# A graph-attention kernel gets its node features in two layouts: projection without transposes, attention columns from raw weights, block table three batches sooner

## The reference

```python
xn = layernorm(x)
xp = (xn @ W).reshape(n, 4, 64)
a_src = einsum('nhc,hc->nh', xp, att_src); a_dst = einsum('nhc,hc->nh', xp, att_dst)
alpha = leaky_relu(a_src[src] + a_dst[dst], 0.2)          # edges, and a loop on each node
w = softmax of alpha over the edges of each target
x = x + elu(segment_sum(xp[src] * w, dst) + bias)
z = layernorm(x)
weights = z @ wr + br                                     # the upper half of the nodes is chosen by it
x = x + z + (chosen ? (gelu(z @ w1 + b1) @ w2 + b2) * weights : 0)
```

## Time and profile before

| | us |
|---|---|
| median of 3 runs | 2629.61 |
| lowest and highest of them | 2623.77 and 2631.42 |
| time of the profiled execution | 2606.92 |
| its span in the trace | 2604.8 |

### The profile page before, as it was taken

How to read it: one execution, slowest core, us unless ns; L and a number is a source line. 1 busy time by engine, 2 the same in 40 slices (tenths; PEclk the granted TensorE clock), 3 DMA queues, 4 the chain that set the end, 5 groups by cost and what they waited for, 6 DMA issues and landing times.

```text
span 2604.8 us, 32956 instructions
## 1 busy us (share of the span) xinstructions
PE 1990.1 (76%) x9573; PEld 1660.8 (64%) x9574; DVE 1581.5 (61%) x3501; ACT 715.3 (27%) x1506; POOL 1570.7 (60%) x1644
## 2 busy tenths in 40 slices
PE   8934878877877777877877877777777787787787
PEld 7723666666666666666666666666666666666665
DVE  4555666665665565665665665665565565565576
ACT  5601232222222222222222222222222222222233
POOL 2366666666666666666666666666666666666630
PEclk9967888888888888888888888988888888888888
DMA  7754444444444444444444444444444444444447
GB/s 240 225 146 121 128 136 124 129 134 127 128 135 126 131 132 127 126 136 125 129 136 126 129 134 125 130 135 129 122 135 133 122 133 131 124 136 124 125 166 302
DMA packets 155904, 364.58 MB, mean 140 GB/s; under 512 B 46725, under 2 KB 74017, under 8 KB 154594
## 3 DMA queue, kind: packets, MB, share of 16 engines
q0 software_dynamic: 76000, 210.72, 29.9%
q1 hardware_dynamic: 72690, 140.11, 16.5%
q10 hardware_dynamic: 7184, 13.41, 1.4%
HBM read 325.22 MB, written 38.89 MB: 140 GB/s over the span
## 4 chain that ended last, share of the span: by engine, by line
POOL 39%; issue 27%; PE 14%; another core or an unknown queue 8%; DVE 5%; POOLq 3%; DMA 2%; ACT 1%; DVEq 0%; SPq 0%; ACTq 0%
POOL rows L664 39%; PE ag_ps L996 7%; PE ag_ps L885 3%; DMA rows<-node_rows,ends 2%; PE y_ps L982 2%; DVE rows L1318 1%; DVE base L1517 1%; POOLq L388 1%; PE h_ps L964 1%; POOLq L684 1%; DVE oh L1278 0%; PE tr_ps L910 0%; PE xl_ps L910 0%; DMA base<-in_x 0%
## 5 line engine op out<-in xcount | busy, mean ns | idle before, releaser
L664 POOL DMA_INDIRECT rows<-node_rows,ends x1582 | 1529.8, 967 | 860.4 <-issue 583.3
L996 PE MATMUL ag_ps<-rows,oh 128*128 128x260 f32 x3518 | 1008.7, 456 | 448.0 <-DVE rows L1318 216.3
L996 PEld LDWEIGHTS ag_ps<-rows,oh 128*128 128x128 f32 x3518 | 808.4, 233 | 618.7 <-issue 275.7
L1318 DVE TENSOR_TENSOR rows<-rows,xl_ps 128x512 f32<-128x512 f32 (+3 forms) x392 | 503.0, 1345 | 29.4 <-issue 17.1
L1297 DVE TENSOR_TENSOR zz<-rows,edge_dm 128x72 f32<-128x72 f32 x98 | 22.8, 233 | 813.6 <-DMA rows<-node_rows,ends 797.6
L964 PE MATMUL h_ps<-xnT,w1s 128*128 128x256 f32 x1568 | 381.3, 392 | 37.2 <-issue 37.0
L790 ACT COPY rows<-rows 128x520 f32<-128x520 f32 x97 | 60.6, 625 | 1261.1 <-DMA rows<-node_rows,ends 1261.1
L964 PEld LDWEIGHTS h_ps<-xnT,w1s 128*128 128x128 f32 x1568 | 307.3, 197 | 93.1 <-issue 50.2
L982 PE MATMUL y_ps<-w2s,hT 128*128 128x256 f32 x1568 | 358.2, 381 | 2.4 <-ACT hT L767 1.7
L982 PEld LDWEIGHTS y_ps<-w2s,hT 128*128 128x128 f32 x1568 | 298.4, 191 | 49.6 <-issue 2.4
L1278 DVE TENSOR_TENSOR oh<-xl_ps,dloc 128x2304 f32<-128x2304 f32 x98 | 250.0, 2551 | 0.0
(11 more groups left out here) (220 smaller groups left out, 1367.7 us busy)
## 6 DMA issues: line engine op xcount, KB each, us to landing
dbc<-dst SPq DMA_DIRECT2D x97, 576.0 KB
rows<-node_rows,ends POOLq DMA_INDIRECT x1582
selfr<-node_rows SPq DMA_DIRECT2D x98, 130.0 KB
base<-in_x SPq DMA_DIRECT2D x14, 896.0 KB, 4.6
base<-in_x SPq DMA_DIRECT2D x49, 256.0 KB
ffn_rows<-yb ACTq DMA_DIRECT2D x48, 256.0 KB
node_rows<-base SPq DMA_DIRECT2D x13, 910.0 KB, 4.8
out<-base SPq DMA_DIRECT2D x4, 896.0 KB, 9.6
```

What stands on the lines that cost most here:

```text
L664: pool.indirect_dma_start(out=rows[:, b, t, :], out_offset=None, in_=table, in_offset=bass.IndirectOffsetOnAxis(ap=ends[:, b, t, 0:1], axi ...
L996: product = nc.tensor.matmul(ag_ps[b][:, 0:ROW], oh[:, b, t, :], rows[:, b, t, :], start=(t == 0), stop=False)
L1318: nc.vector.tensor_tensor(v, v, e, ALU.mult).then_inc(scaled[k], 1)
```

## The change

`x` comes a second time, as `x_turned`: for each batch 128 partitions (features) by 2 halves of 7 x 128 nodes, 7,168 B per partition like the batch of `x`. It has 4 buffers `xt` of its own. PE takes tiles of `xt` as its stationary operand; the transposes and ACT's copies of them are gone. Both loads of a batch count on one semaphore, so DVE and PE wait for both. The load of batch g+4 now waits until PE has projected batch g (`xp_ok`). W and the attention vectors are loaded first. The attention columns are made of the raw W, and `center` then takes the means off all 264 columns; it stands between the statistics and the aggregation of batch 0. The masks move to batches 7 and 8, the counting on PE to the middle of batch 8, the blocks to batch 9, POOL's fetch to its step 10, `window_edges` to batch 11, its sum on PE to the middle of batch 12, the copying out (`first_tiles`) into batch 13. `w1` and `w2` are loaded after the targets of window 0 instead of in batch 10. The batches are written out instead of looped.

```diff
         def _(sp):
             def load_x(g, q):
                 sp.dma_start(xb[q], by_partition(x, g * BATCH, BATCH)).then_inc(x_ld[q], 16)
-
-            load_x(0, 0)
+                sp.dma_start(xt[q], x_turned[:, g, :]).then_inc(x_ld[q], 16)
+
             sp.dma_start(wext[:, :, 0:D], W.rearrange("(c p) n -> p c n", p=P)).then_inc(proj_ld, 16)
             sp.dma_start(att_b[0], bc(att_src.rearrange("h c -> (h c)"), D)).then_inc(att_ld, 16)
             sp.dma_start(att_b[1], bc(att_dst.rearrange("h c -> (h c)"), D)).then_inc(att_ld, 16)
-            for q in range(1, DEEP):
+            for q in range(DEEP):
                 load_x(q, q)
...
-                if not isinstance(g, int) or g + DEEP < NB:
-
-                    wait_apart(sp, (trb_ok, BATCH * (g + 1)), (stat_ok, g + 1))
+                if g + DEEP < NB:
+
+                    wait_apart(sp, (xp_ok, BATCH * (g + 1)), (stat_ok, g + 1))
                     load_x(g + DEEP, q)
-                if isinstance(g, int) and g == NB - DEEP:
-                    load_weights()
+                if g == NB - DEEP:
+                    load_rows_of_weights()
...
             load_targets(0, 0, first)
+            load_weights()
             for b in range(2):
                 sp.wait_ge(tab_st[b], 16 * (NB // 2 + b))
...
                 for t in range(BATCH):
-                    n = BATCH * g + t
-                    act.wait_ge(trb_ok, n + 1)
-                    if known(n, 2):
-
-                        act.wait_ge(xp_ok, n - 1)
-                    nc.scalar.copy(xnT2[:, (b + t) % 2], tr2[(b + t) % 2]).then_inc(trc_ok, 1)
-                    if t >= 1:
-                        row_copy(n - 1, g, t - 1, b, turn)
-                    elif known(g, 1):
-                        row_copy(n - 1, g - 1, BATCH - 1, 1 - b, turn)
-
-            batches(act, batch_copies)
-            row_copy(NW - 1, NB - 1, BATCH - 1, 1, NB // 2 - 1)
+                    row_copy(BATCH * g + t, g, t, b, turn)
...
-            pe.wait_ge(proj_ld, 16)
+            pe.wait_ge(wext_ok, 1)
             for c in range(DC):
-                last = nc.tensor.matmul(y_ps[:, 0:D], ones[:, :], wext[:, c, 0:D], start=(c == 0), stop=(c == DC - 1))
+                last = nc.tensor.matmul(y_ps[:, 0:WIDE], ones[:, :], wext[:, c, :], start=(c == 0), stop=(c == DC - 1))
...
-            def project(n, parity):
-                if isinstance(n, int) and n == 0:
+            def project(n, t, parity, q):
+                if n == 0:
                     pe.wait_ge(wext_ok, 2)
-                pe.wait_ge(trc_ok, n + 1)
-                if known(n, 2):
+                if n >= 2:
                     pe.wait_ge(xpc_ok, n - 1)
                 for c in range(DC):
-                    last = nc.tensor.matmul(ag_ps[parity % 2][:, 0:WIDE], xnT2[:, parity % 2, c, :], wext[:, c, :],
+                    at = (c * BATCH + t) * P
+                    last = nc.tensor.matmul(ag_ps[parity][:, 0:WIDE], xt[q][:, at:at + P], wext[:, c, :],
...
-                    if known(n, 2):
-                        pe.wait_ge(trc_ok, n - 1)
-                    for c in range(DC):
-                        last = nc.tensor.transpose(tr2[(b + t) % 2][:, c, :], xb[q][:, t, c * P:(c + 1) * P], ident[:, :])
-                    last.then_inc(trb_ok, 1)
-                    if known(n, 1):
-                        project(n - 1, b + t - 1)
...
-                wait_apart(dve, (x_ld[q], 16 * (r + 1)), *([(aggr_ok, g)] if known(g, 1) else []))
+                wait_apart(dve, (x_ld[q], 32 * (r + 1)), *([(aggr_ok, g)] if known(g, 1) else []))
                 for t in range(BATCH):
                     last = nc.vector.bn_stats(st_b[:, t, :], xb[q][:, t, :])
                 last.then_inc(stat_ok, 1)
+                if g == 0:
+                    center()
...
-                    for m in {NB - DEEP: [0, 1, 2], NB - DEEP + 1: [3, 4]}.get(g, []):
-                        mask(m)
+                for m in {NB // 2: [0, 1, 2], NB // 2 + 1: [3, 4]}.get(g, []):
+                    mask(m)
...
+                if g == NB // 2 + 4:
+                    window_edges()
+                if g == NB - 1:
+                    first_tiles()
```

More of the change, by code:

```diff
@@ L195, in build @@
         xb = [batch(base_flat, q * BD, D) for q in range(DEEP)]
-        po = [batch(base_flat, DEEP * BD + b * BATCH * WIDE, WIDE) for b in range(2)]
+        xt = [base_flat[:, (DEEP + q) * BD:(DEEP + q + 1) * BD] for q in range(DEEP)]
+        po = [batch(base_flat, 2 * DEEP * BD + b * BATCH * WIDE, WIDE) for b in range(2)]
         dst_all = oh_flat[:, 0:EPP + 1].bitcast(I32)
@@ L356, in two_by_two, with batches @@
                     body(2 * (turns - 1) + b, turns - 1, b)
[L358 to L369, removed]
+        def batches(body):
+            for g in range(NB):
+                body(g, g // 2, g % 2, g // DEEP, g % DEEP)
         def known(n, least):
@@ L608, in rstd_batch @@
             def rstd_batch(g, t, b, r, q):
-                if isinstance(g, int) and g == NB - 1:
+                if g == NB // 2 + 3:
                     pool.wait_ge(block_ok, 1)
@@ L619, in rstd_batch @@
                 nc.gpsimd.tensor_tensor(rs_b[:, b, :], rs_b[:, b, :], minus_half[:, :], ALU.pow).then_inc(rstd_b, 1)
-                if isinstance(g, int) and g == 1:
+                if g == 1:
                     edge_order()
-            batches(pool, rstd_batch, last_peeled=True)
+            batches(rstd_batch)
             pool.wait_ge(const_ok, COUNTED)
@@ L1104, in center @@
                 for c in range(DC):
-                    last = nc.vector.scalar_tensor_tensor(out=wext[:, c, 0:D], in0=y_ps[:, 0:D], scalar=-1.0 / D, in1=wext[:, c, 0:D], op0=ALU.mult, op1=ALU.add)
+                    last = nc.vector.scalar_tensor_tensor(out=wext[:, c, :], in0=y_ps[:, 0:WIDE], scalar=-1.0 / D, in1=wext[:, c, :], op0=ALU.mult, op1=ALU.add)
                 last.then_inc(wext_ok, 1)
@@ L1182, in window_edges, with first_tiles @@
                 nc.vector.tensor_scalar(own_block[0:NW, :], ident[0:NW, 0:NW], length[0:NW, 0:1], None, ALU.mult).then_inc(count_ok, 1)
+            def first_tiles():
+                dve.wait_ge(before_ok, 2)
+                nc.vector.tensor_copy(wi[0:NW, 2:3], lk_ps[0:NW, 2:3])
+                nc.vector.tensor_copy(wi[0:NW, 4:5], lk_ps[0:NW, 3:4]).then_inc(win_ok, 1)
+                then(nc.vector.tensor_tensor(base0_id[:, :], base_id[:, 0:NW], lk_ps[:, P:P + NW], ALU.add))
             constants()
-            batches(dve, batch_stats, last_peeled=True)
-            window_edges()
+            attention_columns()
+            batches(batch_stats)
             keep_asd(NB - 2, 0)
-            dve.wait_ge(before_ok, 2)
-            nc.vector.tensor_copy(wi[0:NW, 2:3], lk_ps[0:NW, 2:3])
-            nc.vector.tensor_copy(wi[0:NW, 4:5], lk_ps[0:NW, 3:4]).then_inc(win_ok, 1)
-            then(nc.vector.tensor_tensor(base0_id[:, :], base_id[:, 0:NW], lk_ps[:, P:P + NW], ALU.add))
             keep_asd(NB - 1, 1)
```

58 lines of the change are left out of this document (28 added, 30 removed).

## The result

The changed kernel takes 2647.97 us (median of 5 runs, 2646.14 to 2657.15), the kernel before 2629.61 (2623.77 to 2633.33). The ratio is 1.0078, 95% interval 1.0066 to 1.009: slower, where 2619.6 was predicted. Its profiled execution has a span of 2647.5 us. That is 42.7 us over the span of the kernel before, but the profiled execution of that one was 22.7 us quicker than the median of its runs; the medians differ by 18.4 us.

What follows compares the result with a forecast made beforehand. PE bounds the opening, then the DMA queue: 24.1 + 72 + 19.5 = 115.6 us on PE, last store 11.0 us sooner, 1 us allowed for held-up gathers; -10.0 us from 2629.6 gives 2619.6, range 2607 to 2633.

Steps and rivals of the forecast that it cites:

- Once the queue is full, each store lands a full round late, ACT waits: Opening: stores queue behind two loads, ACT waits for its output buffer, PE falls to the queue's pace, 7.2 us per batch.
- bytes over the queue's rate plus 0.2 us for gaps: Opening, price of a batch: 6.97 us of transfers plus short gaps, taken as 7.2 us, range 6.97 to 7.5.
- The slower rival: Opening: every batch pays an isolated load's slow beginning, 8.8 us per batch; kernel time 2636 us; chance 10%.
- PE's tile at 0.89 us: Opening, PE: without transposes a tile costs 0.89 us instead of 1.11, so 6.22 us per batch.
- The targets: Start of the opening: ACT's 0.82 MB load of the targets counted within 3.2 MB that passes by 11.8 us.
- Side by side: Opening: loads and stores overlap in the queue, PE's 6.22 us per batch sets the pace; 2611 us; chance 12%.
- one ceiling of 352: Opening: all bytes move at the store's 352 GB/s, 7.86 us per batch; 2626 us; chance 20%.
- 2 x 2.16 + 2.65 = 6.97 us: Opening, DMA queue: two loads at 425 GB/s and one store at 352 GB/s add up per batch.
- The 358 of the Trainium skill: DMA queue: a core's HBM limit of about 358 GB/s, giving a 7.7 us pace and some 5 us gain; not counted on.
- the first projection: Start of the opening, PE: first projection at about 15 us, 3 us later than before.
- batch 0's end: Start of the opening: batch 0 ends on PE at 15.2 + 6.2 + 2.7 = 24.1 us.
- the window table's chain as the last link: End of the opening, SP: table write and read hold the last store until 117.4 us, 1.3 us after the last scaling.

Runs made afterwards that it cites:

- kept-busy version: Changed kernel with four dead projections on PE ahead of the third tile of batches 3, 5, 7 and 9; last table store at 143.13 us against 145.11.
- the version with all cures: Changed kernel with store first, four output buffers, early window table, targets in batch 3, separate load semaphores, earlier small PE products; 2619.58 us against 2629.34 before, ratio 0.9964.

## Why the prediction was wrong

- **"Once the queue is full, each store lands a full round late, ACT waits"** was the step that failed, at the words "full queue" and at the price. I named every link (store, ACT, PE, loads, next store) and then priced a batch as bytes over the queue's rate plus 0.2 us for gaps, which holds only if the loads do not hang on the stores. They do: the loads of batch g+4 are issued when PE ends batch g, and PE cannot end it before the store of batch g-2 has landed. With two buffers this is a closed chain, and the price of a round is the sum over it: 10.96 + 0.49 + 7.39 + 0.76 and gaps, 19.9 us for two batches, 10.0 instead of 7.2. Four buffers open the chain, and the stores' longer landing then costs nothing.
- **The slower rival had the right place and the wrong size.** It stood at 8.8 us a batch, from the slow beginning of an isolated load, and at 10%, because "a full queue shows no such beginning". The missing parts were the store's landing behind 1.84 MB of loads (11 us, where I carried on with bytes over rate) and the clock. Nearest to the measured time was this rival, at 2636, and it too was 12 us short.
- **PE's tile at 0.89 us** was taken as fixed. Behind an idle stretch of 4.5 us it was slower, at a granted clock of 0.50. Batches 2 to 9 took 18.8 us more than forecast. In their four rounds the five tiles behind the wait took 6.83, 7.39, 7.67 and 4.73 us; at 4.73 each it would be 7.7 less. The kept-busy version bears the size out, 2.5 us in each of two rounds. So some 8 of the 18.8 us are the clock, and some 11 the stores' landing and the links beside it.
- **The targets.** ACT stood at the cast until 26.46 us, since 7.3 MB of loads ahead share the engines with the targets' transfer (from 8 to 24 us they move 416 to 433 GB/s; that these loads hold it up is read from the trace, not tested); I had let 3.2 MB pass first. Batch 1 ended 4.4 us late by it, and about 2 of these are the clock once more: PE had stood still for 2.8 us, and its six tiles took 7.32 us, where six at 0.89 are 5.3. It did not matter with two buffers: moved away, the last store came no sooner. With four it did, as the version with all cures shows.
- **Side by side, and one ceiling of 352.** Neither holds: the full queue moved 387 GB/s in one version, 380 in another, 358 in a third (two output buffers with the store first gave 359, close to the ceiling that I had weighed), between the load's 425 and the store's 352. My sum of 2 x 2.16 + 2.65 = 6.97 us stands for 397, more than any version moved. The 358 of the Trainium skill that I weighed is exceeded. The Trainium skill, "HBM Reference", section Specifications (TRN2), says that a core that streams alone goes well above that share, which the 387 bears out.
- **Right** were: the first projection at 15.57 us (15), batch 0's end at 23.9 (24.1), the window table's chain as the last link (2.2 us behind the start of the last scaling, 1.8 forecast), the weights and the attention columns hidden, and the shift of the last store passed on to DVE one for one (17.2 and 17.3 us). That last point is no rule for every version: with all cures 16 us at the last store were 9.8 in time.

## What to carry to other kernels

Where a change adds transfers, don't price them as bytes over a rate before you have followed the ring: which buffer must be free for whom, and when the next load can be issued at all. If the ring closes through the transfer, its round is the sum of all links, and the landing time in it is that of a transfer with its neighbours in flight. In this kernel two more buffers opened the ring: they alone turned the change from 0.8% slower to 0.3% faster, and with an earlier start and the other edits it was 0.4%. The store's place in the queue mattered with two buffers (last store at 123.92 instead of 145) and not with four; a queue of its own did nothing. And an engine that waits in such a ring can come back slower than it left: price its links by the clock that it has after the wait.

## What the runs showed of the hardware

- A store of 0.93 MB issued beside 1.84 MB of loads landed after 11 us, whether it stood behind them in one queue (11.1) or alone in another (11.5); ahead of them it took 8.3. With one load of 0.92 MB a batch it took 5.1 at PE's old pace and 8.4 at the faster one.
- Loads and stores together, without a gap, moved 358 to 387 GB/s at a DMA share of 1.03 to 1.04; the 358 and 359 stand in the two versions with the late start, 380 to 387 in those with the early one and four buffers. What sets the rate between these I did not find out.
- PE's granted clock was 0.50 (the lower of its two levels, 1.2 GHz) behind 4.5 us without a matmul and through most of the five tiles that followed; with PE kept busy in these 4.5 us it stayed at 1.00 (2.4 GHz).
- The same kernel before took 2238 us in two groups of runs and 2605 to 2635 in the others, with the opening the same within 1.4 us where it was compared; so the difference lies in the loop. The gathers themselves take as long (0.96 and 0.97 us), but POOL stands idle before them for 502 us in the one and for 860 in the other (the number behind the second bar of each line), the granted clock is 0.91 and 0.86, and 8% of the second one's chain is put down to "another core or an unknown queue", none of the first one's. No run here says what the cause is.

```profile
L672 POOL DMA_INDIRECT rows<-node_rows,ends x1582 | 1521.4, 962 | 501.7 <-issue 442.6
L664 POOL DMA_INDIRECT rows<-node_rows,ends x1582 | 1529.8, 967 | 860.4 <-issue 583.3
```
